# Row sends of a routed expert layer: four in each of sixteen attention pairs, behind TensorE's output projection, in place of eight in each of eight

## The reference, cut to what matters

```python
def _L1_attn_ref(x, gamma, beta, Wq, Wkv, Wo):
    ...
    q = apply_rope(pos, q)
    k = apply_rope(pos, k)
    ...
    attn = jax.nn.softmax(sim, axis=-1)
    out = jnp.einsum('bhij,bhjd->bhid', attn, v)
    out = out.transpose(0, 2, 1, 3).reshape(b, n, INNER)
    return out @ Wo

def _L1_ffn_ref(x, Wr, br, Wl1, bl1, Wl2, bl2, biases_N):
    ...
    _, idx_BSK = jax.lax.top_k(scores_BSN + biases_N[None, None, :], K)
    ...
    y_NMD = jnp.einsum('nmh,nhd->nmd', jax.nn.silu(a_NMH) * b_NMH, Wl2) + bl2[:, None, :]
    ...
    y_MD = jnp.einsum('mn,nmd->md', ew_MN, y_NMD)
```

## Time and profile before

| | |
|---|---|
| runs | 2482.53, 2477.36, 2473.58 us (median 2477.36) |
| the profiled execution: its own time | 2477.21 us |
| its span in the profile | 2475.4 us |
| granted TensorE clock, mean of the span | 0.956 of 2.4 GHz |
| busy: PE, DVE, ACT, POOL | 2283.6, 1390.1, 936.5, 900.0 us |

### The profile page before, as it was taken

How to read it: one execution, slowest core, us unless ns; L and a number is a source line. 1 busy time by engine, 2 the same in 40 slices (tenths; PEclk the granted TensorE clock), 3 DMA queues, 4 the chain that set the end, 5 groups by cost and what they waited for, 6 DMA issues and landing times. The chain is left out here.

```text
span 2475.4 us, 58172 instructions
## 1 busy us (share of the span) xinstructions
PE 2283.6 (92%) x20696; PEld 1647.3 (67%) x20697; DVE 1390.1 (56%) x3950; ACT 936.5 (38%) x2197; POOL 900.0 (36%) x659
## 2 busy tenths in 40 slices
PE   7999999999997788868899999998899999879996
PEld 5555555556666455655676777776899999746664
DVE  6675333222227756656688877877333333267886
ACT  3211111111125434534566555664222222246663
POOL 4002001544436353654544444442011111147772
PEclk9999999999997788988999999998999999989998
DMA  6013103975446333343333343334666666355552
GB/s 218 17 51 115 39 34 106 267 222 160 124 93 226 96 117 96 96 136 109 103 86 94 87 118 100 95 102 127 237 235 240 240 241 237 108 152 157 146 152 78
DMA packets 163141, 337.64 MB, mean 136 GB/s; under 512 B 25568, under 2 KB 95728, under 8 KB 152656
## 3 DMA queue, kind: packets, MB, share of 16 engines
q1 hardware_dynamic: 142080, 293.37, 37.8%
q0 software_dynamic: 20944, 42.94, 6.7%
HBM read 193.61 MB, written 67.12 MB: 105 GB/s over the span
## 5 line engine op out<-in xcount | busy, mean ns | idle before, releaser
L1671 ACT ACTIVATE at_p<-at_p,at_nmax 128x640 f32<-128x640 f32 (+7 forms) x512 | 393.0, 770 | 207.3 <-DVE at_nmax L1900 206.9
L1900 DVE CUSTOM_DVE_ANT_0 at_p<-at_ps,atk_mask 128x512 f32<-128x512 f32 (+3 forms) x512 | 281.2, 581 | 168.1 <-PE at_ps L1603 108.6
L1918 DVE STREAM_TRANSPOSE at_pB<-at_p 128x512 f32<-128x512 f32 (+3 forms) x512 | 277.0, 584 | 103.5 <-PE at_ps L1624 96.0
L1724 POOL TENSOR_TENSOR kept_big<-kept_xg,atk_cos 128x1024 f32<-128x1024 f32 x64 | 151.7, 2371 | 476.3 <-PE at_ps L1603 438.9
L1603 PE MATMUL at_ps<-kept_big 64*128 64x512 f32 (+3 forms) x1536 | 287.8, 509 | 28.1 <-POOL kept_big L1730 10.5
L1588 PE MATMUL at_ps<-atk_h,atk_w 128*128 128x512 f32 x512 | 242.9, 619 | 19.6 <-SPq L1386 11.9
L1937 DVE SCALAR_TENSOR_TENSOR kept_big<-at_ps,at_inv,kept_big 128x256 f32<-128x256 f32 x512 | 203.9, 474 | 35.5 <-PE at_ps L1645 35.4
L1603 PEld LDWEIGHTS at_ps<-kept_big 64*128 64x128 f32 x1536 | 134.7, 191 | 133.2 <-issue 48.0
L1624 PEld LDWEIGHTS at_ps<-at_pB,at_v_blocks 32*64 32x64 f32 x8192 | 183.3, 134 | 45.9 <-issue 38.7
L1624 PE MATMUL at_ps<-at_pB,at_v_blocks 32*64 32x256 f32 (+1 forms) x8192 | 203.2, 344 | 10.6 <-issue 7.0
L1065 PE MATMUL ex_ps<-kept_big 128*128 128x512 f32 x480 | 208.5, 592 | 0.9 <-ACT kept_big L1122 0.9
(11 more groups left out here) (249 smaller groups left out, 3647.5 us busy)
## 6 DMA issues: line engine op xcount, KB each, us to landing
moe_w<-in_w_w SPq DMA_DIRECT2D x53, 1028.0 KB, 4.3
kept_xg<-kept_xg SPq DMA_DIRECT2D x256, 128.0 KB, 2.3
at_v_blocks<-atk_first_w SPq DMA_DIRECT2D x512, 64.0 KB
atk_first_w<-in_w_w SPq DMA_DIRECT2D x18, 1028.0 KB
atk_w<-in_w_qkv SPq DMA_DIRECT2D x32, 384.0 KB, 3.2
slot_in<-kept_big SPq DMA_DIRECT2D x9, 1032.0 KB
kept_big<-in_w_eg SPq DMA_DIRECT2D x16, 512.0 KB
kept_big<-in_w_eu SPq DMA_DIRECT2D x16, 512.0 KB
```

The lines of the kernel that those rows point to most:

```text
L1671: act.activation(buf, buf, ACT.Exp, bias=nmax[:, unit:unit + 1], scale=-1.0, accum_out=rsum[:, unit:unit + 1]).then_inc(exp_done, 1)
L1724: pool.tensor_tensor(out=out, in0=plain, in1=cos_of, op=ALU.mult).then_inc(cosed, 1)
L1900: ins = dve.tensor_tensor_reduce(out=p[unit % LAG][:, at:to], in0=ring[BANK_OF["S", (t, c), e]][:, 0:to - at], in1=mask[:, 0:CH] if to <= ...
L1918: dve.transpose(strided(pB[e][:, t * P:(t + 1) * P], TURN_STEP, keys), tiles(p[unit % LAG][:, 0:keys * P], keys)).then_inc(turned, 1)
```

## The change

The sends of group j are split in two halves of four, so that they take the sixteen pairs `of` = 1 to 16. With i = `of` - 1, half i belongs to group i // 2. The even halves do what was done once a group before (wait for the sends before, load the rows of a later group, the two small copies, the wait for the loaded rows). All halves then wait until TensorE's W0 of pair i is done (`w_ps`, at least 4 i + 1) and issue four sends. The count of the coming stages' semaphores moves from `of` = 9 to `of` = 17, behind W0 of pair 16. Nothing else is changed: the same 64 sends and 8 loads, the same rows and places.

```diff
-                        j = of - 1
-                        if 0 <= j < TOP * B:
-                            if j == 0:
+                        i = of - 1
+                        if 0 <= i < 2 * TOP * B:
+                            j, first = i // 2, i % 2 * (TB // 2)
+                            at = j // B * NT + j % B * TB
+                            if i == 0:
                                 pool.wait_ge(routed, 1 + ONE)
-                            else:
+                            elif first == 0:
                                 pool.wait_ge(sent, 16 * TB * j)
                                 if j + 1 < TOP * B:
                                     load_rows(j + 1)
-                            at = j // B * NT + j % B * TB
-                            pool.tensor_copy(row_parts(j)[:, :, C], d.tok_w[:, at:at + TB])
-                            pool.tensor_copy(row_parts(j)[:, :, C + 1], number[:, at:at + TB]).then_inc(marked, 1)
-                            pool.wait_ge(marked, j + 1 + ONE)
-                            pool.wait_ge(rows_in[j % 2], 16 * (j // 2 + 1))
-                            for n in range(TB):
+                            if first == 0:
+                                pool.tensor_copy(row_parts(j)[:, :, C], d.tok_w[:, at:at + TB])
+                                pool.tensor_copy(row_parts(j)[:, :, C + 1], number[:, at:at + TB]).then_inc(marked, 1)
+                                pool.wait_ge(marked, j + 1 + ONE)
+                                pool.wait_ge(rows_in[j % 2], 16 * (j // 2 + 1))
+                            pool.wait_ge(w_ps, i * 4 + 1 + ONE)
+                            for n in range(first, first + TB // 2):
                                 pool.indirect_dma_start(out=d.xd, out_offset=bass.IndirectOffsetOnAxis(ap=d.tok_slot[:, at + n:at + n + 1], axis=0),
                                                         in_=rows[j % 2][:, n * ROW:(n + 1) * ROW], in_offset=None).then_inc(sent, 16)
-                        elif j == TOP * B:
+                        elif i == 2 * TOP * B:
+                            pool.wait_ge(w_ps, i * 4 + 1 + ONE)
                             for stage in ("moe", "at2"):
                                 d.signals[stage].count(pool)
```

## The result

The changed kernel takes **2393.91 us** (median of 4 runs, 2393.47 to 2399.68), beside 2475.47 for the kernel before (4 runs). The ratio is 0.967, 95% interval 0.9645 to 0.9701: 82 us faster. Forecast were 2427 us in a range of 2396 to 2463. So the direction was right, the gain was undersized by 33 us, and the time lies 2 us under the range. Of the cases, the small hold (2396 to 2415) is the nearest; its own time, 2396, is 2 us above the measured one.

What follows compares the result with a forecast made beforehand. The prediction took TensorE's signals, late while GpSimd issues sends, to bound the frames with sends. Its sum was 2477.2 - 95.4 + 35.0 + 3.5 + 6.5 = 2426.8, forecast 2427 us, range 2396 to 2463.

Steps and rivals of the forecast that it cites:

- the small hold: Rival for the bursts behind W0: few signals caught, VectorE's slack covers most, 0.3 us a burst; 2396 to 2415 us, chance 0.25.
- The bound: Frames with eight sends: TensorE's signals arrive late while GpSimd issues sends; frames 1 to 6 lose 73.3 us, 12.2 a frame.
- The rule of the Trainium skill: Against the forecast: the 95.4 us have another cause than the sends, and moving them leaves the time near 2477 us.
- Removed, 95.4: Bursts of eight sends gone: frames 1 to 6 give back 73.3 us, frame 0 12.2, frame 8 9.9.
- Fourteen bursts behind W0, 35.0: Bursts of four in halves 0 to 6 and 8 to 14 make VectorE's adds late, 2.5 us each, 35.0 together.
- The pace: Signals behind W0: by frame 8's pace the adds end 1.7 us late, by frame 4's 3.3; 2.5 taken as the middle.
- no hold: Sign that the forecast is wrong: frames with four sends behind W0 stand at 33.6 us instead of near 35.8.
- the forecast case: Bursts of four behind W0 delay VectorE's adds by 1.7 to 3.3 us each; 2415 to 2438 us, chance 0.50.
- The lower bound, 0.3: Least price of a burst behind W0: W1 to W3 all in time, only the wait's own cost, 0.3 us.
- Half 7, 3.5: Frame 8, sends behind the first sequence's end: its loss shrinks from 9.9 us to 3.5 (2 to 5).
- Half 15, 6.5: Sends behind the second sequence's end: SyncE's wait for all sends delays the swap of pair 17; costs 6.5 us (5 to 9).
- The slower rival: Bursts behind W0 idle TensorE and bring its clock down at the scores, 7.9 us each; 2502 us, chance 0.05.

Runs made afterwards that it cites:

- the halving alone: The changed kernel without its two waits on W0, so four sends a pair in sixteen pairs go beside the values products (V1); 2478.70 us, ratio 1.001.

## Why the prediction was wrong, and where it was right

**The bound, right for that chip.** "TensorE's signals arrive late while sends are issued" is borne out: with plain sends at the same place the signals are in time, with spaced ones nearly so, and with the sends elsewhere other signals are late. It is not ScalarE alone that sees them late. In frame 4 of the kernel before, two more engines wait beside it:

```profile
1054.63 1.13 PE L1603 MATMUL at_ps<-kept_big 64*128 64x512 f32 x4
...
1064.95 0.51 SPq L1415 DMA_DIRECT2D at_v<-at_v_next  x1
1065.18 0.69 DVE L1900 CUSTOM_DVE_ANT_0 at_p<-at_ps,atk_mask 128x512 f32<-128x512 f32 x1 [11.26 <-remote]
```

SyncE waits for the same last quarter of V1 as ScalarE's fourth copy and goes at the same time, 1064.95; VectorE waits for the scores S4.0. TensorE itself had gone on to S4.0 at 1054.63, so its work was in time and the news of it was not. Not foreseen was that this belongs to the chip (or the occasion) as well.

The rule of the Trainium skill ("SBUF — State Buffer", section "Who interferes with whom"), that a DMA never contends with a compute engine and TensorE waits for nobody, is about the ports of that memory. The forecast that the prediction drew from it, near 2477, is not borne out where the kernel before takes 2477; on the chips at 2393 and with plain DMAs nothing speaks against the rule. The runs don't show a contention for ports either: late was a signal, of which the section does not speak.

**Removed, 95.4: right.** Frames 1 to 6 lose 73.3 no more, frame 0 went from 55.04 to 43.71, 11.3 where I took 12.2, and frame 8's 9.9 is gone: 94.5. That frame 0 would be near 43.8 without the hold is seen on the chips without late signals too (43.96 in the run with longer rows).

**Fourteen bursts behind W0, 35.0: this step failed.** The twelve in frames 1 to 6 and 9 to 14 cost 4.0 us together, 0.3 each, where 2.5 each was forecast; the two others are within the 11.3 of frame 0 above and the 3.7 of frame 8 below. Even of the 4.0 some 1.6 are not the bursts': frame 1 takes 34.89 us with plain sends on a chip with late signals, and 34.57 to 35.35 in six executions on the chips without. The pace was the error: "W1 and W2 are in at about 3.5 and W3 at about 6.9". I took the first release and the last from bursts beside values products and transposes, and let W3 wait for the end of the burst. W3 was in by 5.1 us after the first send in all these frames but one, and in all seven frames of the version with eight sends behind W0. With VectorE needing W3 at 5.2, the step from "6.9" to "under 5.2" is the step from 1.7 us to nothing. The prediction's own sign of "no hold", frames at 33.6, is what came, though there is a hold: it fell on A0, for which nobody waits closely. Frame 1 shows the forecast case once:

```profile
912.21 1.01 POOL L1786 DMA_INDIRECT slot_in<-kept_big,kept_tok_slot  x1 [7.21 <-PE at_ps L1645]
912.50 4.79 DVE L1941 SCALAR_TENSOR_TENSOR kept_big<-at_ps,at_inv,kept_big 128x256 f32<-128x256 f32 x12
...
918.41 1.66 DVE L1941 SCALAR_TENSOR_TENSOR kept_big<-at_ps,at_inv,kept_big 128x256 f32<-128x256 f32 x4 [1.13 <-issue]
```

Here W3 comes 6.2 us after the first send, VectorE idles 1.13, and the frame is 36.03 long; I had written "near 35.8" for all. The rest of that frame's excess is the 1.6 above. The lower bound, 0.3, was thus about the value, and the rival built on it gave 2396.

Why W1 to W3 get through and other signals don't stays open. The prediction's ground, few and long products "as in frame 8", does not carry it. In frame 8 part of the 2.01 us is no hold (0.56 of it is there on a chip without late signals), but the signal of the second, a long projection, came 3.3 us late: the copy at 1211.95 starts 5.3 us after its products begin, against 2.1 on that chip. S4.0 in the lines above is four long products, and was 9 us late.

**Half 7, 3.5: right**, 3.7 measured; on the chip without late signals it is 2.6 (35.93), so some 1 us of it comes with them. **Half 15, 6.5: right in mechanism, small by 2.1.** Frame 16 of the changed kernel:

```profile
1399.25 0.97 POOL L1786 DMA_INDIRECT slot_in<-kept_big,kept_tok_slot  x1 [0.30 <-issue]
...
1402.71 5.08 SPq L1405 DMA_DIRECT2D kept_xg<-kept_xg  x8
1406.97 2.34 POOL L1727 TENSOR_TENSOR kept_xg<-kept_xg,atk_sin 128x1024 f32<-128x1024 f32 x1 [4.33 <-DMA kept_xg<-kept_xg]
...
1411.93 2.89 PE L1603 MATMUL at_ps<-kept_big 64*128 64x128 f32 x11 [6.85 <-POOL kept_big L1730]
```

The swap goes 3.5 us after the fourth send's start, 7.2 into the frame instead of 0.5 ahead of it: 7.7 later, 7.0 forecast. I took some of it back for a store of `y` out of the way; nothing came back; the 0.9 beyond 7.7 may be the clock, 0.88 in that frame, which was not tried apart.

With these, 2477.2 - 94.5 + 4.0 + 3.7 + 8.6 = 2399.0, against 2399.7 for the profiled execution: what moved is accounted for to within 1 us.

**The slower rival** was right in one thing that the forecast dismissed, that the clock could fall in a wait much shorter than frame 4's 9.90 us. With eight sends behind W0 it did in one of 4.6 us (frame 2, 0.92 over the frame), and with four beside V1 in one of 3.6 (frame 2 of the halving alone, 0.91 over the frame, W taking 5.99 us). It did not matter here, as nothing waits that long behind W0.

**The range** lacked 2 us below: its lower end was the small hold's own time, with nothing left for error under it. The profiled execution of the changed kernel, 2399.7, is inside, but it is the slowest of the four; the median is 5.8 below it, where for the kernel before the profiled execution lay at the median.

## What to carry to other kernels

A lateness read in one place belongs to what stood beside it there. Before moving work to another place, write down for each signal when it is due and when it is needed, and forecast a price near zero where the slack covers the hold. Two parts of a change can be worth nothing or little apart and much together, so price the overlap that each makes possible, here a burst that is over before the next closely awaited signal. Issue indirect DMAs where no engine waits closely for TensorE, or apart from one another, and not just ahead of another queue's wait for all of them. And check a gain on more than one chip.

## What the runs showed of the hardware

Eight indirect sends from GpSimd, 0.97 us each and 1.28 apart, made ScalarE's fourth copy of V1 some 10 us late, waiting for TensorE's signal: traces of three such executions show it, two of them on chips where the kernel before takes 2476 and 2480 us (four of six chips are like that). On the two at 2393 it was in time or at most 0.5 us late, with the same durations of the sends and of V1's matmuls (2.66 us). Plain DMAs of the same rows, 0.54 us each, don't do it on either kind; nor does the size of the rows or their order matter. What differs between the chips, by what path the indirect form holds a signal, and which signals it holds, stays open: no view of the trace shows it.
